# Gated cross-attention and ternary feed-forward on one core: four families of transposes moved from TensorE to transposing DMAs on SyncE

## The reference

```python
def attn(query, key, value, mask):           # 16 heads of 32; mask == 0 -> -1e12
    q, k, v = query @ Wq.T, key @ Wk.T, value @ Wv.T        # split into heads
    return softmax(q @ k.T / sqrt(32)) @ v  @ Wo.T          # heads joined before Wo

def act_quant(a):    # per row, 8 bits
    s = 127 / clip(max(abs(a)), 1e-5)
    return clip(round(a * s), -128, 127) / s

def bitlinear(a, w): # w rounded to -1, 0, 1 times mean(abs(w))
    return act_quant(a) @ weight_quant(w).T

def ffn(a):          # 512 -> 2048 -> 512
    return bitlinear(silu(bitlinear(a, w_gate)) * bitlinear(a, w_up), w_down)

x = x + tanh(g_xattn) * attn(layernorm(x), ctx, ctx, mask)
x = x + tanh(g_ffn) * ffn(layernorm(x))
```

## Time and profile before

| | |
|---|---|
| median of 3 unprofiled runs | 1491.89 us (1491.0 to 1491.93) |
| the profiled execution | 1492.94 us, of which 1491.1 us span |
| mean granted TensorE clock | 0.977 of full speed |
| TensorE matmul busy | 1392.6 us, 93% of the span |
| DVE, ACT, POOL busy | 1063.0, 974.9, 706.1 us |
| DMA | 105.86 MB, 24.2% of the 16 engines' time |

### The profile page before, as it was taken

One profiled execution on the slowest core, in us unless ns is written; L12 is line 12 of the kernel. 1 busy time (PEld: TensorE's weight loads), 2 busy tenths in 40 slices (PEclk: granted clock), 3 DMA queues, 4 the chain that ended last, 5 costly groups with the idle time before them and its releaser, 6 DMA issues.

```text
span 1491.1 us, 29273 instructions
## 1 busy us (share of the span) xinstructions
PE 1392.6 (93%) x9088; PEld 742.1 (50%) x9408; DVE 1063.0 (71%) x2513; ACT 974.9 (65%) x1404; POOL 706.1 (47%) x1187
## 2 busy tenths in 40 slices
...
DMA packets 86885, 105.86 MB, mean 71 GB/s; under 512 B 24366, under 2 KB 58030, under 8 KB 85320
## 3 DMA queue, kind: packets, MB, share of 16 engines
q1 hardware_dynamic: 86856, 105.51, 24.2%
...
## 4 chain that ended last, share of the span: by engine, by line
PE 73%; DVE 11%; ACT 6%; issue 6%; POOL 1%; SPq 1%; DMA 1%; ACTq 0%; DVEq 0%; POOLq 0%
PE bank L1153 22%; PE bank L1175 15%; PE bank L994 7%; PE bank L995 7%; PE bank L996 7%; PE bank L1072 4%; PE bank L1091 2%; PE bank L1164 2%; ACT region L689 2%; PE bank L1103 2%; PE bank L1047 2%; PE bank L1094 1%; ACT up L677 1%; DVE region L942 1%; PE bank L1092 1%
## 5 line engine op out<-in xcount | busy, mean ns | idle before, releaser
L553 POOL TENSOR_TENSOR region<-region,up 128x512 f32<-128x512 f32 x256 | 331.6, 1298 | 353.3 <-DVE region L942 218.0
L1153 PE MATMUL bank<-tern_gate,region 128*128 128x512 fp8e4 x1024 | 264.2, 380 | 5.5 <-DVE region L942 4.7
L1153 PE MATMUL bank<-tern_up,region 128*128 128x512 fp8e4 x1024 | 263.7, 380 | 0.0
L1175 PE MATMUL bank<-tern_down,region 128*128 128x512 fp8e4 x1024 | 231.8, 379 | 11.4 <-ACT region L689 11.4
L544 POOL TENSOR_TENSOR work<-work 124x512 f16<-124x512 f32 x160 | 185.9, 1175 | 100.8 <-ACT work L644 93.3
L942 DVE SCALAR_TENSOR_TENSOR region<-region,bank 128x512 f32<-128x512 f32 x256 | 171.7, 680 | 59.6 <-ACT region L669 59.0
L677 ACT ACTIVATE up<-bank 128x512 f32<-128x512 f32 x256 | 155.1, 606 | 79.7 <-PE bank L1153 79.3
L669 ACT ACTIVATE region<-bank,fs 128x512 f32<-128x512 f32 x256 | 177.0, 692 | 32.2 <-PE bank L1153 30.9
L948 DVE TENSOR_REDUCE hmx<-region 128x1 f32<-128x512 f32 x256 | 167.7, 676 | 5.9 <-POOL region L553 5.9
L681 ACT ACTIVATE region<-region,fs 128x2048 f32<-128x2048 f32 x64 | 128.4, 2006 | 57.1 <-DVE fs L959 57.0
L653 ACT ACTIVATE region<-region,fs 128x512 f32<-128x512 f32 x64 | 46.2, 722 | 180.5 <-DVE fs L935 180.5
...
## 6 DMA issues: line engine op xcount, KB each, us to landing
q_stack<-q_rows SPq DMA_DIRECT2D x96, 256.0 KB, 4.6
xbig<-in_x SPq DMA_DIRECT2D x16, 1024.0 KB, 5.6
q_rows<-q SPq DMA_DIRECT2D x64, 256.0 KB, 2.1
out_y<-o SPq DMA_DIRECT2D x64, 256.0 KB, 2.0
q_stack<-mT SPq DMA_DIRECT2D x32, 256.0 KB, 3.9
region<-in_wgT SPq DMA_DIRECT2D x4, 1024.0 KB, 14.2
region<-in_wuT SPq DMA_DIRECT2D x4, 1024.0 KB, 5.3
region<-in_wdT SPq DMA_DIRECT2D x4, 1024.0 KB, 4.8
```

The source lines that it names most:

```text
L553: nc.gpsimd.tensor_tensor(ht, ht, up[:, n % 2, :], ALU.mult).then_inc(hmul_ready, 1)
L1153: ins = T.matmul(pb[2 * (n % 2) + w][:, :], xqT[:, k, tok], tern[w][:, k * FF + n * GT:k * FF + (n + 1) * GT], start=(k == 0), stop=(k == ...
L1175: ins = T.matmul(pb[2][:, :], hT[:, t % 2, k, :], tern[2][:, k * GT:(k + 1) * GT], start=(k == 0), stop=(k == FK - 1))
```

## The change

The four families of transposes leave TensorE, and so do the ACT copies out of PSUM that belong to them (xT, aT, xq, hT on TensorE and ACT). In their place SyncE issues one transposing DMA for each tile from SBUF to SBUF (`dma_start_transpose`):

- x: ACT makes the high half in f16 from the normalised tile (xh), DVE the low half (xl), both with rows on the partitions; one transfer turns both, 128 x 1024 f16 (tx), 4 a group.
- Attention output: the same for each half of the heads (ah, al; written like xh and xl), one transfer of 128 x 512 f16 (ta), 8 a group.
- Quantised input: after zq ACT subtracts the magic constant and writes bf16 (zb, written like hb), one transfer of 128 x 512 (tz), 4 a group.
- Inner activation: after hq ACT does the same for the tile of 128 x 2048 (hb), one transfer (tH), 4 a group. `hb` is one buffer, `xh`, `ah` and `zb` are two.

The `*_ORDER`, `*_FIRST` and `*_LAST` lists of all five engines are written anew around this (of the lists the diff below shows those of TensorE and SyncE). On TensorE a turn now begins with gu00, and the s, q and wo products use the banks 5, 6, 7, 4 (`WB`). For room in SBUF the identity and some setup scratch move into the buffer `up`, `pace` into `con`, and `fs` shrinks from 16 to 12 columns. The first qs now waits for the second projection weight.

```diff
 TENSOR_ORDER = """
-    F:xq00 A:q00 F:xq10 A:q10 A:q20 A:q30 A:s00 F:gu00 A:s01 F:gu01 A:s10 A:s11 F:gu02 A:s20 A:s21 F:gu03 A:s30
-    A:s31 F:xq20 F:xq30 F:gu10 F:gu11 A:mT00 F:gu12 F:gu13 F:hT00 A:sc00 A:sc01 A:sc02 F:down00 A:sc03 A:sc04
-    F:gu20 F:gu21 A:sc10 A:sc11 A:pv00 F:gu22 A:pv01 F:gu23 A:pv02 F:hT10 A:sc12 A:pv03 A:sc13 A:sc14 A:aT00
-    F:down10 A:aT10 F:gu30 A:pv10 F:gu31 A:pv11 N:xT00 N:xT10 A:pv12 F:gu32 A:pv13 F:gu33 A:aT20 F:hT20 N:xT20
-    N:xT30 A:aT30 F:down20 A:wo00 A:wo10 F:hT30 A:wo20 F:down30 A:wo30
+    F:gu00 A:q00 F:gu01 A:q10 A:q20 F:gu02 A:s00 F:gu03 A:q30 F:gu10 A:s01 A:s10 A:s11 F:gu11 A:s20 A:s21 F:gu12
+    A:s30 A:s31 F:gu13 A:mT00 F:gu20 F:down00 A:sc00 A:sc01 A:sc02 F:gu21 A:sc03 A:sc04 A:sc10 F:gu22 A:sc11
+    A:pv00 A:sc12 A:pv01 F:gu23 A:sc13 A:pv02 F:gu30 A:pv03 A:sc14 F:down10 A:pv10 F:gu31 A:pv11 F:gu32 A:pv12
+    F:gu33 A:pv13 A:wo00 A:wo10 F:down20 A:wo20 A:wo30 F:down30
...
 SYNC_ORDER = """
-    A:qd00 A:qd10 A:qd20 A:qs00 A:qd30 A:kv00 A:m00 A:qs10 F:down00 F:down10 F:down20 A:kv10 A:x00 A:vl00 A:vl10
-    A:vl20 A:vl30 A:vl40 F:down30
+    A:qd00 A:qd10 A:qd20 A:qd30 F:tH00 A:qs00 A:qs10 A:m00 F:tH10 A:ta00 A:ta01 A:ta02 A:ta03 N:tx00 A:ta10
+    A:ta11 F:tH20 F:down00 A:ta12 N:tx10 A:ta13 F:tH30 N:tx20 A:tz00 F:down10 N:tx30 A:x00 A:kv00 A:vl00 A:vl10
+    A:vl20 A:tz10 F:down20 A:tz20 A:vl30 A:vl40 F:down30 A:kv10 A:tz30
 """
...
 SYNC_FIRST = """
-    W:lc00 W:lk00 W:lz00 W:lx00 W:lv00 W:lw00 W:w00 W:w01 W:w02 W:w03 W:lw10 W:ki00 W:lx10 W:kl00 W:w10 W:w11
-    A:qd00 W:vs00 A:qd10 W:w12 W:vl00 W:w13 A:qd20 W:vl10 A:qs00 A:m00 A:qd30 W:vl20 A:qs10 W:vl30 W:vl40 W:w20
-    W:w21 A:kv00 W:w22 W:w23 A:vl00 A:kv10 A:vl10 A:vl20 A:vl30 A:vl40 A:x00
+    W:lk00 W:lc00 W:lz00 W:lx00 W:w00 W:lv00 M:tx00 W:lw00 W:w01 W:w02 M:tx10 W:w03 M:tx20 W:ki00 M:tx30 W:lw10
+    W:kl00 W:w10 W:vs00 A:qd00 A:qd10 W:w11 W:w12 W:w13 W:vl00 A:qd20 W:vl10 A:qd30 W:vl20 A:qs00 A:m00 A:qs10
+    W:lx10 W:vl30 W:vl40 W:w20 W:w21 W:w22 A:ta00 A:ta01 W:w23 A:ta02 N:tx00 N:tx10 A:kv00 A:ta03 A:vl00 A:ta10
+    A:ta11 N:tx20 A:ta12 A:ta13 A:x00 A:kv10 A:vl10 A:tz00 A:tz10 N:tx30 A:vl20 A:vl30 A:tz20 A:vl40 A:tz30
 """
...
+        xh = sb("xh", [P, 2, 2, DM], f16)
+        xT_parts = xT[:, :].bitcast(f16).rearrange("p (c n) -> p c n", c=2 * KC)
+        ah = sb("ah", [P, 2, 2, 2 * P], f16)
+        aT_parts = aT[:, :].bitcast(f16).rearrange("p (c n) -> p c n", c=2 * KC)
+        hb = sb("hb", [P, FF], bf16)
+        zb = sb("zb", [P, 2, DM], bf16)
+        WB = (5, 6, 7, 4)
...
             def q_rows(g, hf, _):
+                if g == 0:
+                    sp.wait_ge(q_weights, 2)
                 sp.wait_ge(q_saved[hf], 16 * 2 * (g + 1))
...
+            def h_transposed(f, t, _):
+                sp.wait_ge(hb_ready, f * TT + (t + 1))
+                if f * TT + t >= 2:
+                    sp.wait_ge(down_mm, f * TT + (t - 1))
+                sp.dma_start_transpose(hT[:, t % 2, :, :], hb[:, :]).then_inc(hT_in[t % 2], 16)
+
+            def x_transposed(g, t, _):
+                sp.wait_ge(xl_ready, g * TT + (t + 1))
+                if g:
+                    sp.wait_ge(q_mm, g * KC)
+                sp.dma_start_transpose(xT_parts[:, :, t * P:(t + 1) * P], xh[:, t % 2, :, :].rearrange("p u d -> p (u d)")).then_inc(xT_in[t], 16)
+
+            def a_transposed(g, hf, t):
+                at = TT * hf + t
+                sp.wait_ge(al_ready, g * (2 * TT) + (at + 1))
+                if g:
+                    sp.wait_ge(wo_mm, (g - 1) * TT + (t + 1))
+                sp.dma_start_transpose(aT_parts[:, 4 * hf:4 * hf + 4, t * P:(t + 1) * P],
+                                       ah[:, at % 2, :, :].rearrange("p u d -> p (u d)")).then_inc(aT_in[hf][t], 16)
+
+            def z_transposed(g, t, _):
+                sp.wait_ge(zb_ready, g * TT + (t + 1))
+                if g:
+                    sp.wait_ge(up_mm, (g - 1) * (TT * FN) + (t + 1) * FN)
+                sp.dma_start_transpose(xqT[:, :, t * P:(t + 1) * P], zb[:, t % 2, :]).then_inc(xq_in[t], 16)
...
+            def x_high(g, t, _):
+                act.wait_ge(xn_ready, g * TT + (t + 1))
+                if t >= 2:
+                    act.wait_ge(xT_in[t - 2], g * 16 + 16)
+                elif not first(g):
+                    act.wait_ge(xT_in[t + 2], g * 16)
+                nc.scalar.activation(xh[:, t % 2, 0, :], xn[:, t % 2, :], ACT.Copy).then_inc(xh_ready, 1)
...
+            def h_integers(f, t, _):
+                act.wait_ge(hq_ready, f * TT + (t + 1))
+                act.wait_ge(hT_in[(t + 1) % 2], f * 32 + 16 * ((t + 1) // 2) + 16)
+                nc.scalar.activation(hb[:, :], h[:, t % 2, :], ACT.Copy, bias=-MAGIC).then_inc(hb_ready, 1)
...
+            def x_low(g, t, _):
+                dve.wait_ge(xh_ready, g * TT + (t + 1))
+                V.tensor_tensor(xh[:, t % 2, 1, :], xn[:, t % 2, :], xh[:, t % 2, 0, :], ALU.subtract).then_inc(xl_ready, 1)
...
-            def h_transpose(f, t, _):
-                pe.wait_ge(hq_ready, f * TT + (t + 1))
-                for half in range(2):
-                    if t < TT - 1:
-                        pe.wait_ge((silu_ready, up_ready)[half], f * (TT * FN) + ((t + 1) * FN + 3))
-                    for k in range(8):
-                        lo = (8 * half + k) * P
-                        ins = T.transpose(pb[half][:, k * P // 2:(k + 1) * P // 2].bitcast(bf16), low_words(h[:, t % 2, lo:lo + P]), ident16[:, :])
-                    ins.then_inc(hT_mm, 1)
-
             def down(f, t, _):
-                pe.wait_ge(hT_ready, f * (TT * 2) + (2 * t + 2))
+                pe.wait_ge(hT_in[t % 2], f * 32 + 16 * (t // 2 + 1) + 16)
```

More of the change, by code:

```diff
@@ L79 @@
[L79 to L82 removed]
+    N:ln00 F:gu00 F:gu01 A:q00 A:q10 A:q20 F:gu02 A:s00 F:gu03 F:hm00 F:hm01 F:hm02 F:hm03 F:hs00 A:q30 A:s01
@@ new lines @@
+    A:s10 F:gu10 A:s11 N:xn00 A:s20 A:s21 F:gu11 A:s30 A:s31 F:gu12 A:mh00 F:gu13 F:hm10 F:hm11 F:hm12 F:hm13
+    F:hs10 F:gu20 F:down00 N:xl00 F:gu21 A:pv00 N:xn10 F:hm20 F:hm21 A:pv01 F:gu22 A:al00 A:al01 N:xn20 A:pv02
+    F:gu23 F:hm22 F:hm23 A:al02 A:pv03 F:hs20 A:al03 F:down10 F:gu30 A:pv10 N:xl10 F:gu31 A:al10 A:pv11 F:hm30
+    A:al11 A:pv12 F:gu32 F:gu33 A:al12 F:hm31 F:hm32 F:hm33 F:hs30 A:wo00 A:pv13 A:st00 A:al13 A:wo10 N:xl20
+    A:zn00 A:st10 N:xn30 A:za00 F:down20 A:zn10 A:wo20 N:xl30 A:za10 A:st20 A:zn20 F:down30 A:wo30 A:st30 A:za20
@@ L128 @@
-    F:gu20 A:sc10 F:gu21 A:sc11 A:pv00 A:sc12 F:gu22 A:pv01 F:gu23 A:pv02 F:hT10 A:pv03 A:sc13 A:sc14 A:aT00
-    F:down10 A:aT10 F:gu30 A:pv10 F:gu31 F:gu32 A:pv11 F:gu33 A:pv12 F:hT20 A:pv13 A:aT20 F:down20 A:aT30 F:hT30
-    A:wo00 A:wo10 A:wo20 F:down30 G:xq00 A:wo30 G:xq10 G:gu00 G:gu01 G:gu02 G:gu03 G:xq20 G:xq30 G:gu10 G:gu11
-    G:gu12 G:gu13 G:hT00 G:down00 G:gu20 G:gu21 G:gu22 G:gu23 G:hT10 G:down10 G:gu30 G:gu31 G:gu32 G:gu33 G:hT20
-    G:down20 G:hT30 G:down30
+    F:gu00 F:gu01 A:q00 F:gu02 F:gu03 A:q10 A:q20 A:s00 A:q30 F:gu10 A:s01 A:s10 F:gu11 A:s11 A:s20 F:gu12 A:s21
@@ L133 @@
+    A:s30 A:s31 F:gu13 F:gu20 A:mT00 F:down00 A:sc00 A:sc01 A:sc02 F:gu21 A:sc03 F:gu22 A:sc04 A:sc10 A:sc11
+    F:gu23 A:pv00 A:sc12 A:sc13 A:pv01 F:gu30 A:sc14 A:pv02 F:down10 A:pv03 F:gu31 A:pv10 F:gu32 A:pv11 F:gu33
+    A:pv12 A:wo00 A:pv13 F:down20 A:wo10 A:wo20 F:down30 G:gu00 G:gu01 G:gu02 G:gu03 G:gu10 G:gu11 A:wo30 G:gu12
+    G:gu13 G:gu20 G:down00 G:gu21 G:gu22 G:gu23 G:gu30 G:down10 G:gu31 G:gu32 G:gu33 G:down20 G:down30
 """
 SCALAR_LAST = """
-    A:q00 F:xq00 A:q10 F:xq10 A:q20 A:q30 F:up00 F:gu00 F:gu01 F:up01 F:up02 F:gu02 F:gu03 F:up03 F:xq20 F:xq30
@@ L146 @@
-    F:hm01 F:hm02 A:mh00 F:gu10 F:hm03 F:hs00 F:gu11 F:gu12 F:hm10 F:gu13 F:down00 F:gu20 F:hm11 F:hm12 F:hm13
-    A:pv00 F:hs10 F:gu21 A:pv01 F:hm20 F:gu22 A:pv02 F:gu23 A:pv03 A:aT00 F:hm21 F:down10 A:aT10 F:hm22 F:gu30
-    A:pv10 F:hm23 F:hs20 F:gu31 F:hm30 A:pv11 F:hm31 F:gu32 A:pv12 F:gu33 A:pv13 F:hm32 F:hm33 F:hs30 A:aT20
-    A:aT30 A:wo00 A:st00 F:down20 A:wo10 A:zn00 A:st10 A:za00 A:wo20 A:st20 A:zn10 A:za10 A:zn20 F:down30 A:wo30
-    A:st30 G:gu00 A:za20 G:gu01 A:zn30 A:za30 G:gu02 G:gu03 G:hm00 G:hm01 G:hm02 G:hm03 G:hs00 G:gu10 G:gu11
```

278 lines of the change are left out of this document (121 added, 157 removed).

## The result

The changed kernel takes 1531.26 us (median of 4 runs, 1529.93 to 1533.59) against 1491.91 us before (4 runs): ratio 1.0264, 95% interval 1.0248 to 1.028. It is 39 us slower, where 1394 us were forecast. The profiled execution took 1531.04 us, its span is 1529.2 us.

What follows compares the result with a forecast made beforehand. TensorE was taken to bound the loop: 15 periods falling from 85.25 to 78.8 us save 96.8 us; with -5 and +4 at the ends, 1492.94 becomes 1395.1, median 1394 us. Own range 1345 to 1440; 8 in 10, 1345 to 1530.

Steps and rivals of the forecast that it cites:

- TensorE as the bound: In the loop, TensorE busy 84.12 of 85.25 us was taken as the bound, beside DVE 62.2 and ACT 57.4.
- neither becomes the bound: ACT at 77% and DVE at 82% of a 76.4 us period: neither would become the bound.
- added waits: TensorE waiting on gu's banks through queues with less slack: 2.4 us a period taken, range nothing to 5 us.
- the 76.4: The loop period in us if 8.8 us of transposes and handoffs go from 85.25, before added waits.
- What leaves TensorE: Transposes of h, attention output, x and quantised input leave: 8.30 us a period, plus 0.5 us of handoffs.
- What the other engines get: Changed copies and low halves per period: ACT to about 58.6 us, DVE to 62.8 us.
- Transfers: SyncE's 20 transposing DMAs a period: 4 us for h, 2.5 us others, 0.4 us issue each, DMAs half busy.
- Do the new chains fit?: Transfers before down and gu have 4.7 to 6 us left on three chains; a 4 us h transfer is hidden.
- The ends: Last FFN -5 us; first turn +4 us from wq's load waiting behind the first transfer of x.
- The transfers that eat the gain (1): Transfers land in 6 to 8 us, down and first gu wait, 5 us more a period: 1460 us; chance 0.10.
- the DMAs as the bound (2): Transfers of h and x land in short pieces, 118 us a period, 1984 us in all; chance 0.18.
- issue per block (3): SyncE pays 0.4 us for every 128 x 128 block, 65 us a period: 1440 to 1530 us; chance 0.08.

Runs made afterwards that it cites:

- a cut of 5.75 us: The kernel before with 8 of the 16 matmuls of each down product left out: 1462.71 us, ratio 0.9802.
- new orders: The changed kernel with value and key loads moved to the next turn and loop-turn and last-turn orders rewritten on all five engines: 1404.43 us, ratio 0.9416.
- run 2: The changed kernel with its four transposing transfers replaced by ordinary copies of the same bytes: 1519.72 us, ratio 1.0178.
- the good orders: The rewritten orders at 1404.43 us; with value and key loads put back where the changed kernel has them, 1433.94 us.
- The exchanges: The changed kernel with neighbours swapped in DVE's order: mh00 earlier 1537.0 us, that plus xn20 later 1519.54 us, xn20 later alone 1517.32 us.

## Why the prediction was wrong, point by point

- **TensorE as the bound, and "neither becomes the bound".** This is where it failed. TensorE was busy 99% of a turn, and its busy time was read as the only limit. In the kernel before, a cut of 5.75 us brought 1.7. I took busy shares of DVE and ScalarE (82% and 77%) for slack and set the added waits at 2.4 us, with 5 as the upper bound. That term of the sum is what was mis-sized. TensorE left the turn with 77.3 us of work, the turn is 85.3 to 86: 8.1 to 8.7 us of idle time, and 8.9 to 9.6 over the 76.4 that I counted from. No single engine's share shows a limit that is made of handoffs; my upper bound was a multiple of a present loss, with no chain behind it. With orders that fit, the turn is 79.1, and 78.8 was forecast; that these agree is partly luck, since those orders are not the change's, and the limit at 78.0 behind TensorE was not in my sum.
- **What leaves TensorE.** 84.1 to 77.3 us busy a turn: right in kind, but 6.85 us where I counted 8.30 (7.4 with new orders). So the 76.4 was too low by itself.
- **What the other engines get.** ScalarE 58.1 us (58.6 forecast), right. DVE 66.4 us against 62.8: the difference is the stalls behind GpSimd, since with the same instructions in other orders it is 62.9; ah, mhl and xn alone make 3.0 of the 3.5 us.
- **Transfers.** h in 3.7 us (4 forecast), the others in 2.3 to 3.1 (2.5), the DMA share 0.47 ("half busy"): right. DMA time added: (0.47 - 0.22) x 85.3 = 21 us, forecast 22. This is an estimated 4.72 MB / 21 us = 220 GB/s, and not the 350 to 400 of the Trainium skill's Advanced Engine Details and Errata, X-Bar Transpose (TRN2). The 1309 ns a block of the Trainium skill's VectorE: DVE Perf Modes, The three transpose paths, are not added up block by block here: 16 blocks of h land in 3.7 us. Issue at 0.4 us: wrong, 1.2 to 1.6 us; with the longer landing it cost at most some 0.5 us an ordinary turn, as run 2 shows.
- **"Do the new chains fit?"** For the transfers in ordinary turns, yes. "Nothing is charged" for SyncE's queue was wrong: I looked at what stands between transfers in an ordinary turn, and passed over the loads of keys and values that are issued there once a batch, some 12 us of issues. They cost 8.3 us in each of three turns, and in the good orders 10. I also asked only whether tz10 comes in time for gu10, which it does; what it is late for is the zb buffer that ScalarE needs before it can begin its next turn.
- **The ends.** Start: +4 forecast; the first load mark comes 2 us earlier. The first transfer goes out at 20.50 us, as said, but the load of wq behind it lands in 5.5 us and not in 11, at 27.4, and its reduction starts at 28.8 instead of 27.1: it was not waited for. The part behind the last load mark is 10.6 us longer instead of shorter; with new orders in it and in its loop turn it is 221.3, 12.5 shorter than before. Of this the last FFN, taken from the start of the last down of the group before to the end, is 66.3 us before, 69.9 in the changed kernel and 64.4 with new orders. So my -5 came as +3.6: in the changed kernel the last down waits 8.8 us for DVE's residual of the tile before, and that one for a buffer whose store stands in SyncE's order behind the last transfer of h, until 1515.47.
- **Rivals.** The transfers that eat the gain (1), the DMAs as the bound (2) and issue per block (3) did not come. The result was slower by a mechanism that no rival named, a chain that the change's own orders lay. Its sign was in my text (a clock under 1.00, TensorE with more gaps), not its cause. Two sums among the ranges are off: the terms named for the low end give 1358 and not 1345, and rival 1 says 5 us a period but multiplies 4.5 (with 5 it is 1469). Neither changes the outcome.

Open: which links close the ring at 83.5 us before and 85.5 after. The exchanges show that a stalled xn20 was one and mh00 not; GpSimd's product is one, by itself or through the stalls of DVE beside it. Whether the old kernel has a shorter turn in other orders wasn't tried; with its transposes on TensorE it can't go under 84.1.
